# Local attention in a fused transformer: the closing feed-forward product moved behind the next trip's first projections

## The reference, cut to what matters

```python
def ffn_layer(x, g, bln, W1, b1, W2, b2):
    mu = x.mean(-1, keepdims=True)
    var = ((x - mu) ** 2).mean(-1, keepdims=True)
    xn = (x - mu) / jnp.sqrt(var + 1e-05) * g + bln
    hg = xn @ W1 + b1
    a, gate = jnp.split(hg, 2, -1)
    return a * jax.nn.gelu(gate, approximate=False) @ W2 + b2
for i in range(DEPTH):      # 6
    x = attn_layer(shift_tokens(x), Wqkv[i], q_scale[i], k_scale[i], Wo[i]) + x
    x = ffn_layer(shift_tokens(x), ln_g[i], ln_b[i], W1[i], b1[i], W2[i], b2[i]) + x
```

## Time and profile before

| | us |
|---|---|
| three timed runs | 4505.05 median, 4504.26 to 4511.89 |
| profiled execution, its own time | 4507.19 |
| its span, first to last instruction | 4505.3 |
| granted TensorE clock over the span | 0.994 |
| busy: PE | 4309.6 (96%) |
| busy: DVE | 3286.9 (73%) |
| busy: ACT | 2757.4 (61%) |
| busy: POOL | 2181.4 (48%) |

### The profile page before, as it was taken

One profiled execution on the slowest core, in us unless ns is written; L12 is line 12 of the kernel. 1 busy time (PEld: TensorE's weight loads), 2 busy tenths in 40 slices (PEclk: granted clock), 3 DMA queues, 4 the chain that ended last, 5 costly groups with the idle time before them and its releaser, 6 DMA issues. The chain is left out here.

```text
span 4505.3 us, 172609 instructions
## 1 busy us (share of the span) xinstructions
PE 4309.6 (96%) x68826; PEld 2563.6 (57%) x68826; DVE 3286.9 (73%) x5789; ACT 2757.4 (61%) x5467; POOL 2181.4 (48%) x1993
## 2 busy tenths in 40 slices
PE   8999999998799999999999999999999999999998
PEld 4555555555455655655555555555555555556554
DVE  5666666665687777777777777777777777777775
ACT  4544555544566666666666666666666666666664
POOL 0000000000366666666666766666766766666763
PEclk9999999999999999999999999999999999999998
DMA  1000000000111112111121112211122111221112
GB/s 44 4 8 6 8 8 4 8 6 4 55 53 51 46 46 71 46 49 50 43 74 48 45 49 61 56 48 47 48 58 59 49 45 48 64 53 49 50 44 80
DMA packets 145061, 189.72 MB, mean 42 GB/s; under 512 B 34151, under 2 KB 66298, under 8 KB 144250
## 3 DMA queue, kind: packets, MB, share of 16 engines
q1 hardware_dynamic: 144250, 178.39, 14.6%
HBM read 29.39 MB, written 4.19 MB: 7 GB/s over the span
## 5 line engine op out<-in xcount | busy, mean ns | idle before, releaser
L1409 POOL TENSOR_TENSOR cs<-cs 128x512 f32<-128x512 f32 x768 | 977.4, 1276 | 534.0 <-DVE cs L1749 531.3
L1535 PE MATMUL psum<-wqkv,xw 128*128 128x512 f32 x2304 | 1191.2, 609 | 24.1 <-DVE tiled L1690 15.6
L1749 DVE TENSOR_TENSOR cs<-psum,rots 128x1024 f32<-128x1024 f32 x768 | 933.8, 1221 | 236.6 <-PE psum L1535 225.5
L1418 POOL TENSOR_TENSOR qk<-cs,rn 128x512 f32<-128x512 f32 x768 | 776.6, 1042 | 330.3 <-ACT rn L1613 294.6
L1629 ACT ACTIVATE sq<-psum 128x512 f32<-128x512 f32 x768 | 459.0, 598 | 623.4 <-DVE cs L1749 591.8
L1442 POOL MEMSET tiled<- 128x128 bf16 x1 | 0.2, 204 | 1165.3 <-POOLq L524 1165.3
L1703 DVE TENSOR_REDUCE ss<-sq 128x8 f32<-128x512 f32 x768 | 520.0, 677 | 7.0
L1479 PEld LDWEIGHTS psum<-pT,vw 64*64 64x64 f32 x18624 | 400.4, 135 | 194.6 <-issue 194.2
L1540 PEld LDWEIGHTS psum<-ident,qk 128*128 128x128 f32 x3088 | 355.2, 141 | 230.6 <-issue 166.8
L1535 PEld LDWEIGHTS psum<-wqkv,xw 128*128 128x128 f32 x2304 | 368.6, 190 | 188.2 <-issue 164.4
L1540 PE MATMUL psum<-ident,qk 128*128 128x128 f32 x3088 | 444.9, 277 | 24.6 <-POOL qk L1418 17.8
(11 more groups left out here) (205 smaller groups left out, 6744.3 us busy)
## 6 DMA issues: line engine op xcount, KB each, us to landing
vw<-vl SPq DMA_DIRECT2D x768, 128.0 KB, 2.4
vw<-vl SPq DMA_DIRECT2D x672, 64.0 KB, 2.0
wqkv<-in_wqkv SPq DMA_DIRECT2D x42, 256.0 KB, 3.8
wol<-in_wol SPq DMA_DIRECT2D x7, 512.0 KB, 4.1
w1l<-in_w1l SPq DMA_DIRECT2D x7, 341.0 KB
xin<-in_x SPq DMA_DIRECT2D x9, 256.0 KB, 2.8
xr<-in_x SPq DMA_DIRECT2D x8, 256.0 KB, 2.8
sums<-sumout SPq DMA_DIRECT2D x8, 256.0 KB, 2.3
```

What stands on the lines that cost most here:

```text
L1409: summed_rot.done(nc.gpsimd.tensor_tensor(own, own, halves(cs[:, t % 2, j, 1, :])[:, :, ::-1, :], ALU.add), at)
L1418: rotated.done(nc.gpsimd.tensor_tensor(qk[:, j, :].rearrange("p (h c) -> p h c", c=EL), cs[:, t % 2, j, 0, :].rearrange("p (h c) -> p h c" ...
L1535: last = nc.tensor.matmul(ps[:, :], xw[:, t * P:(t + 1) * P], wqkv[:, col:col + BANK], start=True, stop=True)
L1749: parts.done(V.tensor_tensor(cs[:, t % 2, j, :, :].rearrange("p i (h c) -> p i h c", c=EL), twice, by_head, ALU.mult), at)
```

## The change

y2 becomes two steps, y2.0 and y2.1. In the loop only y2.0 stands, behind n.0, so behind the four qk.0.j and the four turns of tile 3 of the next trip, and ahead of pt.2.0. It closes the sequence whose hidden values the trip before made. Along with it, t.3.3 stands ahead of qk.0.2, where it stood behind it. In the last part y2.0 stands behind the turns of tile 3, and y2.1, for the last sequence, where y2 stood. Trip 0 has a y2.0 that multiplies zeros: VectorE clears `hf` at the start for that. The loads of `b2l` and `w2l` become `load_closing`, with a semaphore of their own (`w2_loaded`), for which PE waits before y2; at the start they stand between the qkv loads, and in the loop behind the first y2.0 of the second trip of a layer. The other nine loads of the feed-forward weights wait for up.2 instead of y2.

```diff
 BODY = [step(name) for name in """
-    qk.0.0 t.3.0 qk.0.1 t.3.1 t.3.2 qk.0.2 t.3.3 qk.0.3 n.0 pt.2.0 qk.1.0 sa.3
+    qk.0.0 t.3.0 qk.0.1 t.3.1 t.3.2 t.3.3 qk.0.2 qk.0.3 n.0 y2.0 pt.2.0 qk.1.0 sa.3
...
-    up.1 up.2 n.3 o.1.0 o.1.1 y2
+    up.1 up.2 n.3 o.1.0 o.1.1
...
-OF_LAST = (turn(3) + turn_probs(2) + score(3) + final(0) + [("w", 3)] + output(2) + final(1) + final(2) + turn_probs(3) + output(3)
-           + final(3) + [("y",), ("xt",)] + final(4) + [("xn",)] + final(5) + hidden_chunks() + final(6) + [("y2",)] + final(7))
+OF_LAST = (turn(3) + [("y2", 0)] + turn_probs(2) + score(3) + final(0) + [("w", 3)] + output(2) + final(1) + final(2) + turn_probs(3) + output(3)
+           + final(3) + [("y",), ("xt",)] + final(4) + [("xn",)] + final(5) + hidden_chunks() + final(6) + [("y2", 1)] + final(7))
...
-    left = steps("left", last_of("y2", "state"))
+    left = steps("left", place("y2"))
...
+    def closed_at(l, s, which):
+        if which or s > 1:
+            return bass.ds(B - 1 if which else s - 2, 1)
+        past = (l * B + TRIPS - 1) // TRIPS
+        return bass.ds(B - past if s else B - past - past, 1)
+
+    closing_loads = lambda l, s: (l * B + s + B - 2) // B + 1
...
+            def load_closing(layer):
+                sp.dma_start(b2l[:, :], io["b2l"][layer].rearrange("l p -> p l")).then_inc(w2_loaded, 16)
+                at = 0
+                for c, m in enumerate(CW):
+                    sp.dma_start(w2l[0:m, c, :], io["w2l"][layer][:, at:at + m, :].rearrange("l p d -> p (l d)")
+                                 ).then_inc(w2_loaded, 16)
                     at += m
...
-            for j in range(1, 6):
+            for j in range(1, 4):
+                load_qkv(slice(0, 1), j)
+            load_closing(slice(0, 1))
+            for j in range(4, 6):
                 load_qkv(slice(0, 1), j)
...
-                left.wait(sp, it, "state")
+                hidden.wait(sp, it, 2)
                 settle(sp, passed)
                 load_ffn(one)
-                with sp.Fori(1, B - 1) as s:
+                move_values(it + 1, 0)
+                left.wait(sp, it + 1, (0,))
+                settle(sp, passed)
+                load_closing(one)
+                for t in range(1, T):
+                    move_values(it + 1, t)
+                with sp.Fori(2, B - 1) as s:
...
-                if key == ("f", B - 1, 0):
-                    left.wait(pe, it, "state")
+                if key in (("f", B - 2, 0), ("f", B - 1, 0)):
+                    left.wait(pe, it, (at[0] - (B - 2),))
...
-                    hidden.wait(pe, it, 2)
+                    pe.wait_ge(w2_loaded, closing_loads(l, s) * (16 * W2_LOADS))
+                    wait_made(hidden, pe, it, 2, t == 0)
...
-                for dst in (kTl[:, :, :], oTl[:, :, :]):
+                for dst in (kTl[:, :, :], oTl[:, :, :], hf[:, :, :]):
                     V.memset(dst, 0.0).then_inc(made, 1)
-                dve.wait_ge(made, 11)
+                dve.wait_ge(made, 12)
...
-                        out=state[a:b, rest_at(l, s), d:N + d].rearrange("p s n -> p (s n)"), in0=ps[a:b, :],
+                        out=state[a:b, closed_at(l, s, t), d:N + d].rearrange("p s n -> p (s n)"), in0=ps[a:b, :],
                         scalar=b2l[a:b, 0:1], in1=xm[a:b, d:N + d], op0=ALU.add, op1=ALU.add))
-                    left.done(last, "state")
+                    left.done(last, at)
```

20 lines of the change are left out of this document (10 added, 10 removed).

## The result

| | before | after |
|---|---|---|
| timed runs side by side, median | 4506.68 us (4504.26 to 4511.89) | 4592.18 us (4588.97 to 4594.39) |
| ratio | 1 | 1.0188, 95% interval 1.017 to 1.0205 |
| span of the profiled execution | 4505.3 | 4588.9 |
| granted TensorE clock over it | 0.994 | 0.989 |

The kernel is **slower by 85.5 us, 1.9%**; whether that is under or over 2% the interval leaves open. The sign is as predicted, and so is the mechanism within a layer. What happens between layers is not, nor is the size (+55.6 forecast), and the time lies 2 us above the range.

A forecast was written before the change was run, and what follows sets the result against it. PE, busy 96% of the span, was taken as the bound. 42 seams x 1.2 = 50.4, -1.5 between layers and +6.7 at the ends gave +55.6 us on the 4505.05 median: 4560.6 us, range 4515 to 4590.

The forecast's parts named there:

- Parts 1 and 2: Seams within a layer: tile 3's turns held for GpSimd's n.3 products, qk.1.1 1.13 us later; 1.2 us a seam.
- The hold of oa.2: Later in the trip: oa.2 waits for ScalarE's copy of v.0.1, which frees its bank; 0.1 us.
- (a): Seams: cover not needed, n.3's products come 1.8 us sooner and no turn is held; 4448 us, 8%.
- (b): Seams: n.3's products come 1.2 us sooner, hold and gain cancel; 4505 +- 9 us, 4%.
- (c): Pauses at seams let PE's instructions run ahead, shrinking holes among small products; 23.4 us back, 4537 us, 12%.
- (d): The scores' delay carries through the trip, so a seam costs the full 1.97 us; 4593 us, 7%.
- (e): Holds at each seam let TensorE's clock fall to half, 3.4 us a seam more; 4703 us, 2%.
- Part 3: Five seams between layers: the 1.42 us hole overlaps the hold of t.3.0; -0.3 us each, -1.5 in all.
- The rest keeps its distances: Trip behind the head: pauses of VectorE, ScalarE and GpSimd leave its timing unchanged.
- Part 4: The ends: clearing hf 1.3 us, trip 0's added y2.0 1.9, y2.0 in the last part 3.5; sum 6.7.
- Part 5: SyncE's queue: nothing waits for the reordered feed-forward loads; no cost, bounds 0 and 2 us in all.
- the semaphore waits: PE's queue before y2.0: waits for closing weights and hf, long met; nothing, bounds 0 to 0.1 us a seam.

The follow-up runs named there:

- n3_half: The kernel after, with GpSimd's four multiplications for the last tile (n.3) over half the heads each; 4539.1 us, 1.0059.
- third_y2: The kernel before, with y2 cut to the first of its three chunks and nothing moved; 4463.8 us, 0.989.
- cover_once: filled, with y2's six products queued once more for nothing behind o.1.1 in each layer's last trip; 4501.19 us, 0.9976.
- cover_twice: filled, with y2's six products queued twice more for nothing behind o.1.1 in each layer's last trip; 4503.02 us, 0.998.
- up_last_pool: filled, with up.1 and up.2 moved to the trip's end and hf cleared by GpSimd instead of VectorE; 4496.24 us, 0.9967.
- after_pad8: The kernel after, with eight more semaphore increments on TensorE's queue in each trip, ahead of pt.2.0; 4580.72 us, 1.0172.
- filled: The kernel after, with the trip's head reordered so that ready projections and pt.2.0 stand where y2 stood; 4506.66 us, 0.999.

## Why the prediction was right, and where it was wrong

**Parts 1 and 2 (the hold), right.** The turns, y2.0, sa.3 and qk.1.1 stand within 0.12 us of the replay, and n.3's products begin 1.58 us behind the seam's start, as now (1.54). 1.13 a seam was forecast in the head, 1.18 measured. n3_half and third_y2 show the cause from both sides: a shorter product gives 1.28 us a head back, a shorter cover gives 47 us for 82 us of work left out. The hold of oa.2 (0.1 forecast) came at 0.15. Rivals (a), cover not needed, and (b), half-way, are excluded by the same; (c), that the hold feeds PE's instruction supply, too: the holes among the small products are 18.4 + 5.5 us where the earlier trace rows have 12.4 + 11.0. Rival (d), 4593 us, has the measured time but not its mechanism: it wanted the seam to cost the full 1.97, and qk.1.1 came 1.18 later. Rival (a)'s 4448 us comes out of its own terms as 4447 to 4450, by which nothing changes. Rival (e) was priced for every seam; the clock fell, but at the returns, where the cost was not looked for.

**Part 3 (the returns), the step that failed.** The prediction read the earlier trace rows as a hole of 1.42 us behind y2 and kept the hole at that size when y2 went, so that qk.0.0 would come 2.68 us sooner and win. The hole is what y2 left over of a fixed way back: a branch of 3.4 to 4.0 us that is issued when y2's products are queued, not when they are done. Taking y2 away brought qk.0.0 only 0.50 us sooner (4.50 to 4.00), and 2.68 us of y2 were added to the head: +2.12 instead of -0.3, outside the bounds of -1.3 and +0.5, and 12 us over the five. The branch stood in the trace of before, with 3.61 us as its median; the prediction looked only at the engine's idle time. y2 had thus a second cover to give, and the diff took both. The half clock behind the returns is a second price, 1.75 us each by cover_once; in after it is partly hidden, because late projections meet GpSimd's products when they are ready (the head there is 16.96, below the usual 17.46).

The Trainium skill, "Runtime: NRT & Kernel Launch", section "Instruction fetch mechanics", says that a taken branch breaks the sequential prefetch and, where its target isn't in the two pages at hand, stalls until the target's page is fetched. The durations of the branch, 3.4 to 4.0 us taken and 0.08 not, agree, though no run shows the fetch itself. That queued products run on meanwhile is shown by cover_twice. The prediction had that section beside it and used it for (c) only.

The Trainium skill, "TensorE: Matmul & The Clock Gate", section "HAM oscillation — how this bites in real kernels", has idle gaps bring the clock down; the returns of after (3.5 to 4.1 us idle) agree, and the prediction gave it to every seam or none. At the returns of all runs, the clock stayed up where the idle time was 1.8 us or less, and fell where it was 3.4 us or more; between 2.3 and 3.4 us it mostly fell, but in up_last_pool only at three of the five. It has also fallen without such a return: at 4248 us in after, at three places in after_pad8.

**The rest of the trips, mis-sized.** "The rest keeps its distances" cost nothing beyond 3 us in the sum; it took 13.5. A part seems to shift with instructions elsewhere (after_pad8, -0.21 us a trip); the cause is open. It is no hold of n.3's products: n3_half has 51.60, filled 51.57.

**Part 4, right in kind: 5.3 us for 6.7.** Clearing hf: 1.3 forecast, 1.6 measured, since 0.27 us of idle time stands ahead of its 1.34. Trip 0's head 2.3 for 1.9. The last part +1.4 for 3.5: y2.0's instructions stood 0.45 us apart, at full clock, where the earlier trace rows had half; the moment at which the clock falls had moved. **Part 5** as forecast: nothing waits for the loads. The 5 us of the start that are not the change's were in no term, and could not be; without them the profile would give +78.6. If the timed runs have them too, the time would have been inside the range without them, by luck, with the step of part 3 as wrong.

**The range.** Its upper end was set just short of (d). The forecast's own upper end of 4582 us doesn't come out of its terms: 42 x 1.6 + 5 x 0.5 + 1.3 + 1.9 + 5.1 + 2 = 80 gives 4585, and 4589 with the 0.1 a seam for the semaphore waits, both still below the measured time. The returns' bounds were too narrow, and the rest of the trips had no bound of its own although 47 trips multiply whatever it does: 0.1 us there is 5 us.

## What to carry to other kernels

Before work is moved away from where an engine is waited for, ask what it covers, and count every cover: here one product hid both GpSimd's multiplications and the loop's way back, and the second was only visible as a branch on the queue and a small hole behind it. A hole without a releaser behind queued work has a length that depends on that work, so work it out from where the branch is issued. A moved step wants other ready work in its place (filled: 15.30 against 17.46 us), and here the loop on TensorE ended best in long queued products, even useless ones (cover_once, 0.9976 against 0.999).

## What the runs showed of the hardware that was not expected

- The way back to a loop's start on TensorE's queue: 3.4 to 4.0 us as the branch is taken, 0.08 at the exit. It overlaps with twelve queued instructions (5.2 us), which then leave no idle time at all (cover_twice). The weights' transfers lengthen it where they are issued 1.5 us ahead of it: 4.58 to 5.38 us with their bytes and 3.92 to 4.33 without.
- Six useless products at each return made the kernel faster than without (4501.19 against 4506.66 us; to the kernel before 0.9976 [0.9967, 0.9985] against 0.999 [0.998, 0.9999]), by holding the clock (1.00 instead of 0.50 behind each return).
- Eight more increments per trip on TensorE's queue left after no slower and its profiled span 13 us shorter.
- The stretch ahead of the changed code has two levels in the profiles, about 5 us apart, for kernels that are the same up to there; the upper level goes with a second stretch at half clock, 10.2 or 13.7 us long.
